# Scores and bias of a unit's first head group issued one slot earlier, and an output projection that waits half by half

## The chip, the cores and the metric

The kernel runs on one core of a Trainium2 chip. The metric is the device time of one execution in microseconds (us). Five engines run streams of their own and meet at semaphores: TensorE (PE, its weight loads are shown as PEld), VectorE (DVE), ScalarE (ACT), GpSimd (POOL) and SyncE (SP, which issues the transfers here).

## The reference, cut to what matters

Two attention layers stand one after the other, over 64 batch elements of 128 rows and 512 columns, with 16 heads of 64, one shared key and value head, a null key and value, a causal mask, and a layer norm before the projections and behind the output projection:

```
xn = layernorm(x) * g_in                       # 128 x 512
q = xn @ Wq ; k, v = xn @ Wkv                  # layer 1: q and k brought to unit length and scaled
sim = q @ concat(null_k, k).T + bias           # bias: a given tensor (layer 0), a small network (layer 1)
attn = softmax(where(causal and mask, sim, -big))
x = x + layernorm((attn @ concat(null_v, v)) @ Wo) * g_out
```

Layer 1 takes the x that layer 0 leaves.

## The kernel before, in words

A *unit* is one batch element in one layer; there are 128. The order of the work is written out by hand, for each engine apart, as a row of *slots*, one unit `u` each. In the slot of `u` the engines do: scores, softmax and values of `u`; the output projection and output norm of the unit before, `v`; the input projections of a later unit or pair of units, `w`; the input statistics of a still later one, `n`. `then` is the unit whose slot comes next. Layer 0's units are projected in pairs, layer 1's one by one. The steady state is a loop of 29 rounds with four slots in each (one more round of the same four stands behind it, then six slots of layer 1's kind):

- `first`: u of layer 1, project the first half of the heads of a layer-0 pair w (`project_pair(w, 0, ...)`);
- `late`: u of layer 0, project one layer-1 unit w (`project`, then `transpose_k`, `transpose_q`);
- `second`: u of layer 1, project the keys and the second half of the heads of the pair;
- `late` again.

The names that the steps below need:

- `scores(u, c)` (L643 on, matmul L673): the scores of head group c (0 or 1) into the PSUM banks `SB[c]`. `SB[0]` is the two banks `Y` and `XT`, which also take the output projection and the transposed input; so the transposes (L543) and `project_out(v, 0, u)` (L708) that come behind wait for `biased[0]`.
- `add_bias(u, c)` (DVE, L1128): adds the masked bias to the scores of group c, from PSUM into `probs`, and raises `biased[c]`. Only then is the bank free.
- `row_max` (DVE, L1134), `exponential` (ACT, L896), `inverse_sum` (DVE, L1139), `divide` (POOL, L1466), `turn` (DVE, L1144): the softmax, in two groups of row blocks; `turned[1]` is its end.
- `values(u)` (matmul L690): 64 small matmuls (32-row tiles) in four steps k, behind `turned`.
- `split_o` on ACT (L902, two halves `o_hi`) and on DVE (L1151, two halves `o_lo`): values out of PSUM. `project_out(v, p)` has three passes of eight matmuls: p = 0 and 1 read `o_hi`, p = 2 reads `o_lo`.
- `take_half` (ACT, L866): copies half of a pair's projected queries from PSUM into `qp` and raises `half_copied`. A layer-0 unit's scores read `qp`.
- `rstd_of_input` (ACT, L835 and L837), `input_statistics` (DVE, L1068, L1070), `normalise` (DVE, L1075), `split_x` (ACT L848 or L850, DVE L1081 or L1083: high and low parts of the transposed input), `centre_output` (DVE, L1156 to L1160), `mask_bias` (POOL, L1456).

Before the change each slot begins on PE with `scores(u, 0)`, `scores(u, 1)`, and on DVE with `add_bias(u, 0)`, `add_bias(u, 1)`.

Of the kernel before, what the change touches and what calls it, by code (L numbers as in the profile page):

```python
# [139 lines left out]
BLOCKS = 4  # L140
# [20 lines left out]
def build(nc, x, bias0, null_kv, keep0, keep1, L0, L1, out):  # L161
# [18 lines left out]
    with ctx:  # L180
# [358 lines left out]
        def _(pe):  # L539
# [137 lines left out]
            def values(u):  # L677
                n, filled = side(u)
                wait(pe, v_rep_loaded[n], filled * 16 * 4)
                wait(pe, o_lo_done[1], u.prev)  # L680
                for g in range(len(GROUPS)):
                    wait(pe, turned[g], u.done)
                if not isinstance(u.done, int):
                    pe.sem_inc(pe_passed, 1)
                p_t = probs_t[:, :, :, :, :].rearrange("p (c e) k b i -> p c e k b i", e=2)
                for k in range(BLOCKS):
# [6 lines left out]
                m.then_inc(values_done, 1)  # L693
# [46 lines left out]
            def begin(w, n, n2, then):  # L740
# [8 lines left out]
                transpose_v(w)  # L749

            def first0(u, v, w, n, then):
                scores(u, 0)
# [9 lines left out]
                values(u)  # L762

            def second0(u, v, w, n, then):
                pe.wait_ge(diag_computed, 1)
                scores(u, 0)
# [10 lines left out]
                values(u)  # L777

            def late0(u, v, w, n, loads, then, pairs_done):
                pe.wait_ge(lo_done, 3 * KC)  # L780
                pe.wait_ge(bias1_copied, BLOCKS)
# [3 lines left out]
            def first(u, v, w, n, then):  # L785
                scores(u, 0)
# [7 lines left out]
                values(u)  # L794

            def second(u, v, w, n, then):
                scores(u, 0)
# [7 lines left out]
                project_pair(w, 1, (3,), u)  # L805
                wait(pe, pair_v_ready, w.pdone * 2)
                values(u)

            def late(u, v, w, n, loads, then, pairs_done):
                if u:  # L810
                    scores(u, 0)
                    scores(u, 1)
# [11 lines left out]
                if u:  # L824
                    if not w:
                        wait(pe, o_lo_done[0], u.prev)
                    values(u)
# [4 lines left out]
        def _(act):  # L832
# [220 lines left out]
        def _(dve):  # L1053
# [70 lines left out]
            def add_bias(u, c):  # L1124
                if c == 0:
                    wait(dve, masked_bias_done, u.done)
# [125 lines left out]
            def begin(w, n, n2, then):  # L1252
# [312 lines left out]
```

## Time and profile before

| | |
|---|---|
| median of 3 runs | 2237.0 us (2236.79 to 2238.55) |
| the profiled execution's own time | 2237.55 us, its span 2235.8 us |
| busy in the span | PE 93%, PEld 83%, DVE 73%, ACT 70%, POOL 46% |
| granted TensorE clock | 0.989 of full speed |
| a round of four slots, from the transposes of one `first` to those of the next | 67.51 us (1064.08 to 1131.59) |

Busy time is summed over the execution, so a share says how much of the span an engine worked, not whether it was waited for. PE's records overlap by their pipelined ends; the idle times that the views put beside an instruction are counted from the end of the one before.

### The profile page before, as it was taken

Reading aid. Unit: us, or ns where it says so; the run is one execution under the profiler, and the core shown is the slowest. Engines: PE = TensorE matmul, PEld = TensorE weight load, DVE = VectorE, ACT = ScalarE, POOL = GpSimd, SP = SyncE. Lnnn points to the kernel's source line nnn. Section 1 sums busy time; section 2 is a strip of 40 time slices with the busy share of each in tenths; the row PEclk is TensorE's granted clock in tenths of the full one; section 3 lists DMA queues with packets and bytes.
Section 4 is the critical chain, followed back from the end, with each engine's and each line's share of the span. In section 5 each row is a group of like instructions: output and inputs, shape, how many; then the busy total and the mean of one; then the engine's idle time right before and its main releaser. Section 6 shows DMA issues by size and latency. Waiting matters only on the chain.

```text
span 2235.8 us, 72261 instructions
## 1 busy us (share of the span) xinstructions
PE 2077.9 (93%) x26395; PEld 1859.0 (83%) x26395; DVE 1625.1 (73%) x3422; ACT 1562.1 (70%) x6241; POOL 1028.6 (46%) x1510
## 2 busy tenths in 40 slices
PE   4799999999999999999999999999999999999987
PEld 4788888888888888888888888888888888888876
DVE  5677777777777777777777777777777777777775
ACT  4567777777777677776777776676677677677775
POOL 3444444444544544544444444444444444444453
PEclk8899999999999999999999999999999999999998
DMA  8112222212222212222222221122221122221111
GB/s 257 41 55 61 70 61 61 67 55 60 72 61 61 67 55 60 72 61 61 62 59 61 72 61 56 58 68 59 69 64 55 57 68 61 63 68 58 59 59 45
DMA packets 183034, 147.47 MB, mean 66 GB/s; under 512 B 121440, under 2 KB 125616, under 8 KB 182992
## 3 DMA queue, kind: packets, MB, share of 16 engines
q1 hardware_dynamic: 181248, 145.77, 21.8%
q0 software_dynamic: 688, 1.14, 0.3%
q8 instruction: 26, 0.43, 0.1%
q10 hardware_dynamic: 1056, 0.00, 0.0%
q14 instruction: 16, 0.13, 0.0%
HBM read 98.56 MB, written 37.77 MB: 61 GB/s over the span
## 4 chain that ended last, share of the span: by engine, by line
PE 62%; DVE 16%; DMA 6%; issue 5%; ACT 4%; SPq 3%; POOL 2%; DVEq 0%; POOLq 0%; ACTq 0%
PE psum L708 21%; PE psum L581 15%; PE psum L615 11%; DVE probs L1128 6%; PE psum L690 6%; PE psum L673 4%; DMA xa<-in_x_dram 4%; ACT probs L896 4%; DVE neg_max L1134 2%; POOL probs L1466 2%; SPq L443 2%; PE psum L592 2%; DVE o_lo L1151 2%; DMA v_kept<-v_diff 2%; DVE bn_in L1068 2%
## 5 line engine op out<-in xcount | busy, mean ns | idle before, releaser
L896 ACT ACTIVATE probs<-probs,neg_max 128x129 f32<-128x129 f32 (+3 forms) x2048 | 712.7, 352 | 66.7 <-DVE neg_max L1134 66.7
L1456 POOL TENSOR_TENSOR masked_bias<-bias,pad_neg 128x516 f32<-128x516 f32 (+3 forms) x512 | 403.9, 821 | 220.1 <-DVE probs L1128 214.1
L1466 POOL TENSOR_TENSOR probs<-probs,den_inv 128x512 f32<-128x512 f32 (+3 forms) x512 | 368.0, 740 | 214.2 <-DVE den_inv L1139 214.1
L1478 POOL TENSOR_TENSOR y_out<-y_out,res 128x512 f32<-128x512 f32 x128 | 164.7, 1287 | 538.0 <-ACT y_out L860 538.0
L896 ACT ACTIVATION_READ_ACCUMULATOR probs<-probs,neg_max 128x1 f32 x2048 | 386.7, 189 | 0.0
L1144 DVE STREAM_TRANSPOSE probs_t<-probs 128x512 f32<-128x512 f32 (+3 forms) x512 | 230.0, 487 | 138.3 <-POOL probs L1466 137.2
L708 PE MATMUL psum<-wo_hi,o_hi 128*128 128x512 f32 x1024 | 275.3, 411 | 19.9 <-DVE probs L1128 18.5
L1128 DVE TENSOR_TENSOR probs<-psum,masked_bias 128x648 f32<-128x648 f32 x256 | 201.5, 828 | 118.3 <-PE psum L673 118.0
L708 PE MATMUL psum<-wo_hi,o_lo 128*128 128x512 f32 x1024 | 264.9, 400 | 21.0 <-DVE o_lo L1151 21.0
L708 PE MATMUL psum<-wo_lo,o_hi 128*128 128x512 f32 x1024 | 260.6, 396 | 0.0
L708 PEld LDWEIGHTS psum<-wo_hi,o_lo 128*128 128x128 f32 x1024 | 187.5, 188 | 77.1 <-DVE o_lo L1151 25.9
L1134 DVE TENSOR_REDUCE neg_max<-probs 128x4 f32<-128x516 f32 (+3 forms) x512 | 233.8, 483 | 13.4
L708 PEld LDWEIGHTS psum<-wo_hi,o_hi 128*128 128x128 f32 x1024 | 186.5, 192 | 58.8 <-issue 17.4
L708 PEld LDWEIGHTS psum<-wo_lo,o_hi 128*128 128x128 f32 x1024 | 192.0, 188 | 41.4
L902 ACT ACTIVATE o_hi<-psum,null_v_col 128x512 fp32r<-128x512 f32 x256 | 162.1, 684 | 45.8 <-PE psum L690 40.7
L690 PE MATMUL psum<-probs_t,v_rep 32*64 32x256 f32 (+3 forms) x8192 | 183.9, 308 | 8.8 <-DVE probs_t L1144 8.7
L866 ACT COPY qp<-psum 128x512 f32<-128x512 f32 x128 | 74.3, 582 | 164.6 <-PE psum L581 164.6
L1151 DVE SCALAR_TENSOR_TENSOR o_lo<-psum,null_v_col,o_hi 128x512 fp32r<-128x512 f32 x256 | 187.3, 741 | 1.8 <-ACT o_hi L902 1.8
L690 PEld LDWEIGHTS psum<-probs_t,v_rep 32*64 32x64 f32 x8192 | 156.5, 132 | 38.3 <-issue 20.3
L581 PE MATMUL psum<-xp_hi,w_hi 128*128 128x256 f32 x1024 | 168.6, 286 | 5.6 <-ACT w_hi L934 4.3
L615 PE MATMUL psum<-w_hi,x_hi 128*128 128x384 f32 x768 | 167.0, 339 | 0.0
L615 PE MATMUL psum<-w_lo,x_hi 128*128 128x384 f32 x768 | 166.8, 339 | 0.0
(133 smaller groups left out, 3986.8 us busy)
## 6 DMA issues: line engine op xcount, KB each, us to landing
res<-in_x_dram SPq DMA_DIRECT2D x64, 256.0 KB, 2.7
v_rep<-v_kept SPq DMA_DIRECT2D x512, 32.0 KB, 1.8
x_of<-y_out SPq DMA_DIRECT2D x64, 256.0 KB, 2.1
res<-x_of SPq DMA_DIRECT2D x64, 256.0 KB, 2.7
out_dram<-y_out SPq DMA_DIRECT2D x64, 256.0 KB, 2.1
xa<-in_x_dram SPq DMA_DIRECT2D x63, 256.0 KB, 2.7
xa<-x_of SPq DMA_DIRECT2D x63, 256.0 KB, 2.9
q_aside<-qp SPq DMA_DIRECT2D x32, 256.0 KB, 3.1
```

The costliest lines, as they stand in the source:

```text
L581: m = nc.tensor.matmul(o, ws[0][:, c, q:q + P], xs[:, c, :, :].rearrange("p b i -> p (b i)"), start=(n == 0), stop=(n == 3 * KC - 1))
L615: m = nc.tensor.matmul(Q[b][:, 0:hi - lo], xs[:, c * P:(c + 1) * P], ws[1][:, c, lo:hi], start=(n == 0), stop=(n == 3 * KC - 1))
L690: m = nc.tensor.matmul(o, v_rep[n][strip, k, :], p_t[strip, :, e, k, k:, :].rearrange("p c b i -> p c (b i)"), start=(k == 0), stop=(k == ...
L708: m = nc.tensor.matmul(Y[:, 0:D], os[:, k * P:(k + 1) * P], ws[u.layer][:, j, :], start=(p == 0 and k == 0), stop=(p == 2 and k == PAIRS - 1))
L896: x_ = nc.scalar.activation(s, s, ACT.Exp, bias=neg_max[:, b, n:n + 1], accum_out=den[:, b, n:n + 1])
L1128: nc.vector.tensor_tensor(pairs(probs, c), SB[c][:, :, 0:ROW], pairs(masked_bias, c), ALU.add).then_inc(biased[c], 1)
L1134: nc.vector.tensor_reduce(neg_max[:, b, :], block(probs, b), AX.X, ALU.max, negate=True).then_inc(max_done[b], 1)
L1144: m = nc.vector.transpose(probs_t[:, :, 0:b + 1, b, :], block(probs, b)[:, :, 1:].rearrange("p n (k r) -> p n k r", r=R))
L1151: nc.vector.scalar_tensor_tensor(part_of(o_lo), psum[:, 4 + 2 * f:6 + 2 * f, 0:2 * P], null_v_col[:, 0:1], part_of(o_hi).bitcast(F32), ALU ...
L1456: m = nc.gpsimd.tensor_tensor(block(masked_bias, b), block(bias[u.layer], b), pad_neg[u.layer][:, 0:WIDTH[b]].unsqueeze(1).to_broadcast([P ...
L1466: m = nc.gpsimd.tensor_tensor(some, some, den_inv[:, b, :].unsqueeze(2).to_broadcast([P, 4, n]), ALU.mult)
L1478: nc.gpsimd.tensor_tensor(y_out[:, :], y_out[:, :], res[:, :], ALU.add).then_inc(out_done, 1)
```

## The change

PE: `scores(then, 0)` is issued in the slot before that of its unit: in `first` and `second` ahead of `values(u)`, in `late` between the second and the third of the four steps of `values(u)`. A slot then begins with `scores(u, 1)`. `project_out` waits for the first half of `o_hi` or `o_lo` ahead of its first matmul and for the second half ahead of its fifth.

DVE: `add_bias(then, 0)` is the last instruction of the slot before (with waits for `turned`, since it overwrites `probs`). In `first` the two `split_o` come ahead of the last two `row_max`; in `second` the second `split_o` comes ahead of the last `row_max`.

ACT: in `first`, `split_x(w.even)` comes ahead of `rstd_of_input(w.odd)`.

```diff
             def project_out(u, p, now=None):
+                arrived = {0: o_hi_done, 2: o_lo_done}
                 if p == 0:
-                    for b in range(2):
-                        wait(pe, o_hi_done[b], u.done)
                     wait(pe, y_taken, u.prev)
                     if now:
                         wait(pe, biased[0], now.done)
-                if p == 2:
-                    for b in range(2):
-                        wait(pe, o_lo_done[b], u.done)
                 for k in range(PAIRS):
                     j = k // 2 + 4 * (k % 2)
+                    if p in arrived and k % 4 == 0:
+                        wait(pe, arrived[p][k // 4], u.done)
...
             def first(u, v, w, n, then):          # PE
-                scores(u, 0)
                 scores(u, 1)
...
                 project_pair(w, 0, (0, 1, 2, 3), u)
-                values(u)
+                scores(then, 0)
+                values(u, range(BLOCKS))
...
             def second(u, v, w, n, then):         # PE
-                scores(u, 0)
                 scores(u, 1)
...
                 project_pair(w, 1, (3,), u)
+                scores(then, 0)
                 wait(pe, pair_v_ready, w.pdone * 2)
-                values(u)
+                values(u, range(BLOCKS))
...
             def late(u, v, w, n, loads, then, pairs_done):   # PE
-                    scores(u, 0)
                     scores(u, 1)
...
-                    values(u)
+                    values(u, range(2))
+                if then:
+                    scores(then, 0)
+                if u:
+                    values(u, range(2, BLOCKS))
...
             def first(u, v, w, n, then):          # ACT
+                split_x(w.even)
                 rstd_of_input(w.odd)
-                split_x(w.even)
...
             def add_bias(u, c):                   # DVE
                 if c == 0:
+                    for g in range(len(GROUPS)):
+                        wait(dve, turned[g], u.prev)
                     wait(dve, masked_bias_done, u.done)
...
             def first(u, v, w, n, then):          # DVE; second and late lose and gain the same add_bias
                 input_statistics(w.odd)
-                add_bias(u, 0)
                 add_bias(u, 1)
...
                 split_x(w.even)
+                split_o(v, 0)
+                split_o(v, 1)
                 row_max(u, 2)
                 row_max(u, 0)
-                split_o(v, 0)
-                split_o(v, 1)
...
                 normalise(n)
+                add_bias(then, 0)
```

The start-up slots (`begin`, `first0`, `second0`, `late0`) are changed in the same way.

PE where a `late` slot ends and the next begins, before: four steps of values (L690), then both groups of scores (L673).

```order
L690 MATMUL psum<-probs_t,v_rep 64x256 x8
L690 MATMUL psum<-probs_t,v_rep 64x2x96 x8
L690 MATMUL psum<-probs_t,v_rep 64x2x64 x8
L690 MATMUL psum<-probs_t,v_rep 64x2x32 x8
L673 MATMUL psum<-keys,q_t 64x129 x4
L673 MATMUL psum<-keys,q_t 64x97 x4
L673 MATMUL psum<-keys,q_t 64x65 x4
L673 MATMUL psum<-keys,q_t 64x33 x4
L673 MATMUL psum<-keys,q_t 64x129 x4
L673 MATMUL psum<-keys,q_t 64x97 x4
L673 MATMUL psum<-keys,q_t 64x65 x4
L673 MATMUL psum<-keys,q_t 64x33 x4
```

The same place after the change (values are L691 there).

```order
L691 MATMUL psum<-probs_t,v_rep 64x256 x8
L691 MATMUL psum<-probs_t,v_rep 64x2x96 x8
L673 MATMUL psum<-keys,q_t 64x129 x4
L673 MATMUL psum<-keys,q_t 64x97 x4
L673 MATMUL psum<-keys,q_t 64x65 x4
L673 MATMUL psum<-keys,q_t 64x33 x4
L691 MATMUL psum<-probs_t,v_rep 64x2x64 x8
L691 MATMUL psum<-probs_t,v_rep 64x2x32 x8
L673 MATMUL psum<-keys,q_t 64x129 x4
L673 MATMUL psum<-keys,q_t 64x97 x4
L673 MATMUL psum<-keys,q_t 64x65 x4
L673 MATMUL psum<-keys,q_t 64x33 x4
```

The first group of the next unit's scores now stands in the middle of the values.

PE at the end of `second`, before, with the semaphores waited for: the last tile of the pair's projection (L581), the values, then the scores of the next unit, of layer 0, which wait for the copied queries.

```order
L581 MATMUL psum<-xp_lo,w_hi 128x8x32 x4
L64 REGISTER_ALU
L64 ISA [waits pair_v_ready]
L690 MATMUL psum<-probs_t,v_rep 64x256 [waits turned1,turned0,v_rep_loaded2,o_lo_done1]
L690 MATMUL psum<-probs_t,v_rep 64x256 x7
L690 MATMUL psum<-probs_t,v_rep 64x2x96 x8
L690 MATMUL psum<-probs_t,v_rep 64x2x64 x8
L690 MATMUL psum<-probs_t,v_rep 64x2x32 x8
L64 REGISTER_ALU [waits half_copied1,half_copied0]
L673 MATMUL psum<-kv_t,qp 64x129 [waits k_high_loaded,y_taken]
```

After the change (the scores go on for 13 more matmuls, and the values stand behind them).

```order
L581 MATMUL psum<-xp_lo,w_hi 128x8x32 x4
L64 REGISTER_ALU
L64 REGISTER_ALU [waits half_copied1,half_copied0]
L673 MATMUL psum<-kv_t,qp 64x129 [waits k_high_loaded,y_taken]
L673 MATMUL psum<-k_high,qp 64x129
L673 MATMUL psum<-kv_t,qp 64x129
```

The wait for `half_copied` now comes directly behind the projection whose result is copied, and no longer behind the values.

DVE at the beginning of `first`, before.

```order
L1128 TENSOR_TENSOR probs<-psum,masked_bias 128x648 [waits scores_done0,masked_bias_done]
L1128 TENSOR_TENSOR probs<-psum,masked_bias 128x648 [waits scores_done1]
L1134 TENSOR_REDUCE neg_max<-probs 128x4 [waits biased1,biased0]
L1075 TENSOR_SCALAR xn<-xa,mv_in,rstd_in 128x512 [waits xt_done,rstd_in_done]
L1134 TENSOR_REDUCE neg_max<-probs 128x4
L1083 TENSOR_TENSOR xp_lo<-psum,xp_hi 128x4x128 [waits x_hi_done]
L1134 TENSOR_REDUCE neg_max<-probs 128x4 x2
L64 REGISTER_ALU
L1151 SCALAR_TENSOR_TENSOR o_lo<-psum,null_v_col,o_hi 128x512 [waits o_hi_done0]
L1151 SCALAR_TENSOR_TENSOR o_lo<-psum,null_v_col,o_hi 128x512 [waits o_hi_done1]
```

After the change (add_bias is L1134, row_max L1140, normalise L1079, split_x L1087, split_o L1157).

```order
L1134 TENSOR_TENSOR probs<-psum,masked_bias 128x648 [waits scores_done1]
L1140 TENSOR_REDUCE neg_max<-probs 128x4 [waits biased1,biased0]
L1079 TENSOR_SCALAR xn<-xa,mv_in,rstd_in 128x512 [waits xt_done,rstd_in_done]
L1140 TENSOR_REDUCE neg_max<-probs 128x4
L1087 TENSOR_TENSOR xp_lo<-psum,xp_hi 128x4x128 [waits x_hi_done]
L64 REGISTER_ALU
L1157 SCALAR_TENSOR_TENSOR o_lo<-psum,null_v_col,o_hi 128x512 [waits o_hi_done0]
L1157 SCALAR_TENSOR_TENSOR o_lo<-psum,null_v_col,o_hi 128x512 [waits o_hi_done1]
L1140 TENSOR_REDUCE neg_max<-probs 128x4 x2
```

One addition has left the beginning of the slot, and the two `o_lo` stand ahead of the last two maxima.

## Rows read from the trace of the kernel before

**Rows 1.** Page: the span, then busy time, share and instructions of each engine.

```profile
span 2235.8 us, 72261 instructions
PE 2077.9 (93%) x26395; PEld 1859.0 (83%) x26395; DVE 1625.1 (73%) x3422; ACT 1562.1 (70%) x6241; POOL 1028.6 (46%) x1510
```

**Rows 2.** Page: the chain of work that ended last, shares by engine.

```profile
PE 62%; DVE 16%; DMA 6%; issue 5%; ACT 4%; SPq 3%; POOL 2%; DVEq 0%; POOLq 0%; ACTq 0%
```

**Rows 3.** Waits, PE: us in total, times, longest.

```profile
PE psum L543 <- DVE probs L1128: 53.3, 94, 7.2
...
PE psum L708 <- DVE o_lo L1151: 21.0, 30, 0.9
...
PE psum L708 <- DVE probs L1128: 18.5, 32, 3.6
```

**Rows 4.** Timeline, PE, slot `first`: start, us, instruction, count, [idle before, releaser].

```profile
1062.11 1.44 PE L673 MATMUL psum<-keys,q_t 64*64 64x129 f32 x64 [0.50 <-issue]
1064.08 0.65 PE L543 MATMUL psum<-ident,xn 128*128 128x128 f32 x4 [0.53 <-DVE probs L1128]
...
1068.31 0.60 PE L543 MATMUL psum<-ident,xn 128*128 128x128 f32 x4
1069.69 2.11 PE L708 MATMUL psum<-wo_hi,o_lo 128*128 128x512 f32 x8 [0.79 <-DVE o_lo L1151]
...
1077.41 1.42 PE L690 MATMUL psum<-probs_t,v_rep 32*64 32x256 f32 x64
```

**Rows 5.** Timeline, PE, end of `second` and beginning of `late`.

```profile
1109.74 0.64 PE L581 MATMUL psum<-xp_hi,w_lo 128*128 128x256 f32 x4
1110.21 0.63 PE L581 MATMUL psum<-xp_lo,w_hi 128*128 128x256 f32 x4
1110.77 1.42 PE L690 MATMUL psum<-probs_t,v_rep 32*64 32x256 f32 x64
1112.17 0.29 PE L673 MATMUL psum<-kv_t,qp 64*64 64x129 f32 x1
...
1112.78 0.30 PE L673 MATMUL psum<-kv_t,qp 64*64 64x129 f32 x1
...
1114.08 0.65 PE L543 MATMUL psum<-ident,xn 128*128 128x128 f32 x4 [0.47 <-DVE probs L1128]
```

**Rows 6.** Timeline, ACT, end of the same `second`.

```profile
1110.79 0.29 ACT L835 ACTIVATE ln_in<-mv_in,eps_col 128x1 f32<-128x1 f32 x1 [1.20 <-DVE mv_in L1070]
...
1111.22 0.57 ACT L866 COPY qp<-psum 128x512 f32<-128x512 f32 x1
```

**Rows 7.** Timeline, PE, window of 0.06 us around the last matmuls of those values.

```profile
1111.87 0.32 PE L690 MATMUL psum<-probs_t,v_rep 32*64 32x64 f32 x6
```

**Rows 8.** Timeline, DVE, slot `first`.

```profile
1062.10 0.70 DVE L1068 BATCH_NORM_STATS2 bn_in<-xa 128x6 f32<-128x512 f32 x1 [0.25 <-DMA xa<-in_x_dram]
...
1063.12 1.57 DVE L1128 TENSOR_TENSOR probs<-psum,masked_bias 128x648 f32<-128x648 f32 x2
...
1065.41 1.24 DVE L1075 TENSOR_SCALAR xn<-xa,mv_in,rstd_in 128x512 f32<-128x512 f32 x1
...
1067.49 0.74 DVE L1134 TENSOR_REDUCE neg_max<-probs 128x4 f32<-128x388 f32 x2
1068.15 1.39 DVE L1151 SCALAR_TENSOR_TENSOR o_lo<-psum,null_v_col,o_hi 128x512 fp32r<-128x512 f32 x2
...
1075.38 0.74 DVE L1144 STREAM_TRANSPOSE probs_t<-probs 128x384 f32<-128x384 f32 x2
```

**Rows 9.** Timeline, DVE, ACT and PE, end of a `late` slot and beginning of `second`.

```profile
1095.09 0.75 DVE L1160 SCALAR_TENSOR_TENSOR y_out<-y_out,mv_out,g_out 128x512 f32<-128x512 f32 x1
...
1095.76 1.27 ACT L902 ACTIVATE o_hi<-psum,null_v_col 128x512 fp32r<-128x512 f32 x2
...
1095.64 1.44 PE L673 MATMUL psum<-keys,q_t 64*64 64x129 f32 x64
1097.58 2.12 PE L708 MATMUL psum<-wo_hi,o_hi 128*128 128x512 f32 x8 [0.50 <-DVE probs L1128]
```

More of the change, by code:

```diff
@@ L675, in scores, with values @@
                 m.then_inc(scores_done[c], 1)
-            def values(u):
+            def values(u, blocks):
                 n, filled = side(u)
[L679 to L684, printed above, removed]
+                if 0 in blocks:
+                    wait(pe, v_rep_loaded[n], filled * 16 * 4)
+                    wait(pe, o_lo_done[1], u.prev)
+                    for g in range(len(GROUPS)):
+                        wait(pe, turned[g], u.done)
+                    if not isinstance(u.done, int):
+                        pe.sem_inc(pe_passed, 1)
                 p_t = probs_t[:, :, :, :, :].rearrange("p (c e) k b i -> p c e k b i", e=2)
-                for k in range(BLOCKS):
+                for k in blocks:
                     for e in range(2):
@@ L692, in values @@
                                                  start=(k == 0), stop=(k == BLOCKS - 1))
-                m.then_inc(values_done, 1)
+                if BLOCKS - 1 in blocks:
+                    m.then_inc(values_done, 1)
             def project_out(u, p, now=None):
+                arrived = {0: o_hi_done, 2: o_lo_done}
                 if p == 0:
-                    for b in range(2):
-                        wait(pe, o_hi_done[b], u.done)
                     wait(pe, y_taken, u.prev)
@@ L793, in first @@
                 project_pair(w, 0, (0, 1, 2, 3), u)
-                values(u)
+                scores(then, 0)
+                values(u, range(BLOCKS))
             def second(u, v, w, n, then):
-                scores(u, 0)
                 scores(u, 1)
@@ L805, in second @@
                 project_pair(w, 1, (3,), u)
+                scores(then, 0)
                 wait(pe, pair_v_ready, w.pdone * 2)
-                values(u)
+                values(u, range(BLOCKS))
             def late(u, v, w, n, loads, then, pairs_done):
                 if u:
-                    scores(u, 0)
                     scores(u, 1)
@@ L826, in late @@
                         wait(pe, o_lo_done[0], u.prev)
-                    values(u)
+                    values(u, range(2))
+                if then:
+                    scores(then, 0)
+                if u:
+                    values(u, range(2, BLOCKS))
             run_units(pe, begin, first0, second0, late0, first, second, late, NB)
@@ L1125, in add_bias @@
                 if c == 0:
+                    for g in range(len(GROUPS)):
+                        wait(dve, turned[g], u.prev)
                     wait(dve, masked_bias_done, u.done)
@@ L1304, in first0 @@
                 low_parts((2 * KC + 1,))
+                add_bias(then, 0)
             def second0(u, v, w, n, then):
                 low_parts((2 * KC + 2,))
-                add_bias(u, 0)
                 add_bias(u, 1)
@@ L1326, in second0 @@
                 low_parts((2 * KC + 3, 3 * KC))
+                add_bias(then, 0)
             def late0(u, v, w, n, loads, then, pairs_done):
@@ L1334, in first @@
                 input_statistics(w.odd)
-                add_bias(u, 0)
                 add_bias(u, 1)
@@ L1352, in first @@
                 normalise(n)
+                add_bias(then, 0)
             def second(u, v, w, n, then):
-                add_bias(u, 0)
                 add_bias(u, 1)
@@ L1360, in second @@
                 row_max(u, 2)
+                split_o(v, 1)
                 row_max(u, 0)
-                split_o(v, 1)
                 inverse_sum(u, 0)
@@ L1371, in second @@
                 normalise(n)
+                add_bias(then, 0)
             def late(u, v, w, n, loads, then, pairs_done):
                 if u:
-                    add_bias(u, 0)
                     add_bias(u, 1)
@@ L1412, in late @@
                 centre_output(v)
+                if then:
+                    add_bias(then, 0)
             run_units(dve, begin, first0, second0, late0, first, second, late, NB)
```

4 lines of the change are left out of this document (2 added, 2 removed).

## The prediction

> **What bounds the kernel now.** I read the page first: PE is busy for 2077.9 of 2235.8 us [rows 1], and the chain that ended last runs 62% over PE and 16% over DVE [rows 2]. So PE sets the time, and 158 us of its idle time are all that a change of order can win. The list of waits says who causes the part that this change touches: 53.3 us of transposes waiting for the bias addition in 94 waits, 18.5 us of output projections waiting for it in 32, and 21.0 us of output projections waiting for `o_lo` in 30 [rows 3]. The longest of the first two lists, 7.2 and 3.6 us, lie in the start-up slots. Without them 46.1 us in 93 and 14.9 us in 31 are left, 0.49 us at each slot's beginning, four times a round; the `o_lo` wait comes once a round, in `first`.
>
> The timeline shows how it arises. In `first`, the scores begin at 1062.11 and are all issued and finished by 1063.55, but the transposes behind them start at 1064.08, 0.53 us later, because the addition for group 0 must first clear the banks [rows 4]. Later in that slot the third output pass starts 0.79 us late [rows 4], since DVE ran the two `o_lo` only from 1068.15 to 1069.54 [rows 8].
>
> **Removed.** With `add_bias(then, 0)` done before the slot begins, the waits at slot beginnings go: 46.1 + 14.9 = 61.0 us. That needs DVE to be in time. At a `late` slot's end the last instruction of the output norm ends at 1095.84 [rows 9]; an addition behind it takes about 0.8 (1.57 for two [rows 8]), so `biased[0]` comes at about 1096.7, while the output pass started at 1097.58 before [rows 9] and is wanted at about 1097.4 after. The cover is some 0.5 us.
>
> A stall costs a little more than its idle row, since a stream of matmuls overlaps: between groups of one kind the next starts before the recorded end of the last (1109.74 + 0.64 = 1110.38, next at 1110.21, so 0.17), and where the tile shape changes by 0.07 (1110.21 + 0.63 = 1110.84, values at 1110.77) [rows 5]. So 124 beginnings give 124 x 0.07 = 8.7 us more, and 30 `o_lo` waits 30 x 0.17 = 5.1.
>
> For the `o_lo` wait I lay out the slot after, with T the start of its transposes. DVE first ends the moved addition, then needs 1.02 us for the input statistics (1062.10 to 1063.12, [rows 8]). PE meanwhile issues the last two steps of the values, crosses the loop's branch (0.50 [rows 4]) and issues the second group of scores (0.61, from 1112.17 to 1112.78, [rows 5]), so DVE starts `add_bias(u, 1)` at about T + 0.25 and ends it at T + 1.05. From there row_max takes 0.72 (1064.69 to 1065.41), then normalise, one row_max and split_x 2.08 (1065.41 to 1067.49) and the two `o_lo` 1.39 [rows 8]. The first `o_lo` is ready at T + 4.55, the second at T + 5.25. PE wants the first at T + 4.66 (the odd transposes at T + 4.23, as from 1064.08 to 1068.31, and 0.60 less the overlap of 0.17 for them [rows 4]) and the second four matmuls later, half of a pass of 2.11 - 0.17 [rows 4], at T + 5.6. Both are just in time, the first by 0.1 us. I take the whole 21.0 us; the other bound is nothing.
>
> Sum removed: 61.0 + 21.0 + 8.7 + 5.1 = 95.8 us.
>
> **Added.** *Changes of tile shape.* Scores use 64-row tiles, values 32-row, the rest 128. `first` and `second` gain one change each (scores alone ahead of the values), a `late` slot two (scores amid the values): six a round, 180 in 30 rounds, some 12 more in the single `late` slots, 192. The projection's groups start 0.47 us apart, the values start 0.56 behind the last of them [rows 5]: a change costs 0.09. From values to scores: six matmuls are in flight from 1111.87 [rows 7]; 64 in 1.40 us is 0.02 each, so the last is issued near 1111.97, and the scores start at 1112.17 [rows 5]: 0.20, less 0.02, is 0.18, with the scores' own waits in it. From scores to values no row stands; I take 0.13 for all, midway, with ends of 0.09 and 0.20. 192 x 0.13 = 25 us.
>
> The Trainium skill (TensorEngine Tiling (Array Packing), Key Properties) speaks against the change here: it says that a change of tiling mode drains TensorE. The trace agrees that a change costs something but shows the next matmul 0.07 us ahead of the last one's recorded end [rows 5]. A full drain at each change is among the rivals.
>
> *A new wait in `second`.* This is the part that the change does to itself. `scores(then, 0)` for a layer-0 unit needs the second `take_half`, which ACT can only begin when PE has finished the last projected tile. Before, the values hid it: they were issued at 1110.77, and ACT ended the copy at 1111.22 + 0.57 = 1111.79 [rows 5, 6]. ACT is also held until 1110.79 by the statistics of another unit, which it takes first [rows 6]. Now PE stands until about 1111.85 (0.06 for the signal, as the statistics' release to ACT): 1.08 us, with the values, `split_o` and the next slot queued behind. Nothing else of PE can slip in. 31 x 1.08 = 33.5 us.
>
> *The half-wise wait.* It matters where no transposes stand between: `late` to `second`. ACT began `o_hi` 0.12 us behind the first score (1095.64, 1095.76) and takes about 0.68 for a half of its 1.27 [rows 9]; with 0.06 the half is ready 0.86 behind the values, and the second group of scores covers 0.61 + 0.15. 0.10 x 30 = 3 us. A wait for both halves would have cost 0.6 more each; so the split of the waits is needed, and that of `o_lo` likewise.
>
> DVE, ACT and POOL get no new work. The start-up waits should shrink by two additions, about 2 us (bounds nothing and 10.8).
>
> **Sum.** 95.8 - 25 - 33.5 - 3 + 2 = 36 us, 1.2 us of a round of 67.5. The profiled execution took 2237.55, 0.55 above the median of the runs; against the median of 2237.0 that gives **2201 us**.
>
> **Rivals.**
> *The new wait stays away* (ACT copies earlier because its statistics come earlier): + 33.5, 2168. For it: ACT waits 1.20 us for DVE's statistics there [rows 6]. Against: those wait for the transposed v of the same projection, and no line of `second` on ACT moves.
> *DVE is late in `first`*: the margin of 0.1 us is less than what one stretched instruction costs (normalise took 1.24 us here beside POOL's bias [rows 8]). If the wait for `o_lo` or for `split_x` stays as long as it was, 26 us are not won: 2227; half of it gives 2214.
> *A full drain at each change of shape*: the last small matmul of the values takes 0.22 (six in 0.32, 0.02 apart [rows 7]); 192 x (0.22 - 0.02) is 38 us in place of 25: 2214. That is what the Trainium skill's sentence on mode switching (TensorEngine Tiling (Array Packing), Key Properties), taken strictly, would come to.
> *Slower: the softmax of `first` ends too late.* `turn` ended at 1075.38 + 0.74 = 1076.12 [rows 8], and the values came at 1077.41 [rows 4], 1.29 us of cover. After the change exponentials start 0.4 us later behind T (the addition's end at T + 1.05 against 1064.69 - 1064.08 = 0.61), PE comes 0.96 earlier and 0.74 later by the scores ahead of the values: 0.7 us of cover. From 0.7 us of delay PE waits for `turned`; from 1.85 the gain is gone; 2.5 would give 30 x 0.65 = 20 us more than before, 2257. For it: two maxima now stand behind `o_lo`. Against: ACT reaches them only after eight exponentials of group 0.
> *No effect*: gains and new waits cancel (every small bound at its bad end): 2233 to 2241.
>
> **How the numbers follow.** My forecast has a chance of 0.52; new wait absent 0.08; DVE late 0.14; full drain 0.14; cancelled 0.05; slower 0.07. Within 0.2% of the median, about what a measurement of this kernel can tell, is 2232.5 to 2241.5: faster 0.88, same 0.05, slower 0.07. The range leaves out the slower case, the cancelled one and the far end of the absent wait: 2170 to 2226.
>
> **What would show it.** Right: the idle times for the bias addition at slot beginnings are gone or below 0.1 us, so is the one for `o_lo`; in `second` one new wait of PE's scores on ACT's copy (L866 of before), about 1.1 us, 30 times; a round of about 66.3 us. The values' group in `late` is longer by its two changes, 0.2 to 0.4. Wrong: a wait of the values on `turn`, of the odd transposes on `split_x`, or of slot beginnings on the bias addition as before; or no wait on the copy.

## The result, and the profile after

The changed kernel takes 2399.4 us (median of 4, 2398.89 to 2401.68) against 2237.6: a ratio of 1.0725, interval 1.0706 to 1.0744. That is 162 us more, where the forecast had been 36 us less (2201). The profiled execution has a span of 2397.1 us.

The page after: span, busy time of the engines, and the queue that carries instructions (packets, MB, share of the 16 DMA engines). Before, that queue had 26 packets and 0.43 MB.

```profile
span 2397.1 us, 72132 instructions
...
PE 2148.4 (90%) x26395; PEld 1914.7 (80%) x26395; DVE 1624.3 (68%) x3422; ACT 1557.8 (65%) x6241; POOL 1030.0 (43%) x1510
...
q8 instruction: 278, 4.55, 0.9%
```

The list of PE's waits after (us in total, times, longest), beside [rows 3]:

```profile
PE psum L673 <- issue: 153.8, 58, 5.0
PE psum L673 <- ACT qp L870: 42.0, 30, 4.4
...
PE psum L708 <- ACT o_hi L906: 1.5, 4, 0.9
...
PE psum L543 <- DVE probs L1134: 1.1, 2, 0.7
```

The three waits of [rows 3] are gone, as meant: 53.3 us in 94 is 1.1 in 2, and the two rows of L708 on `o_lo` and on the bias addition stand no more. The predicted new wait on ACT's copy is there: less its start-up case, 42.0 - 4.4 = 37.6 us in 29, 1.30 each. But one row that nobody had moved has grown from 14.2 us in 29 to 153.8 in 58: scores that wait for "issue", for nothing that the profile shows. Before, it read

```profile
PE psum L673 <- issue: 14.2, 29, 0.9
```

The timeline of PE after, in the slot `first`, beside [rows 4]:

```profile
1064.84 1.07 PE L673 MATMUL psum<-keys,q_t 64*64 64x129 f32 x32 [4.63 <-issue]
1065.84 1.11 PE L543 MATMUL psum<-ident,xn 128*128 128x128 f32 x4
1066.61 3.05 PE L708 MATMUL psum<-wo_hi,o_hi 128*128 128x512 f32 x8
1069.49 2.02 PE L708 MATMUL psum<-wo_lo,o_hi 128*128 128x512 f32 x8
...
1071.71 2.11 PE L708 MATMUL psum<-wo_hi,o_lo 128*128 128x512 f32 x8
```

This is the loop's restart. It cost 0.50 before [rows 4] and costs 4.63 now. The transposes then take 1.11 us in place of 0.65, the first output pass 3.05 in place of 2.11. The windows of PE (length, busy times with instructions in brackets, granted clock, DMA share, GB/s) say why: of two whole rounds and of two stretches of the second of them,

```profile
985.84:1059.86 74.02, 67.26 (x840) 59.99 (x833) 49.75 (x106) 47.92 (x194) 31.53 (x46) 0.95 0.21 59
1059.86:1132.91 73.05, 66.03 (x840) 59.03 (x832) 49.83 (x105) 47.93 (x194) 31.61 (x46) 0.98 0.21 59
1059.86:1065.00 5.14, 0.51 (x37) 0.40 (x25) 1.61 (x3) 1.87 (x3) 1.53 (x2) 1.00 0.12 36
1065.00:1070.00 5.00, 5.00 (x47) 4.27 (x43) 3.49 (x6) 2.98 (x14) 3.05 (x4) 0.66 0.27 81
```

PE stood nearly idle for 5 us, and the granted clock of the 5 us behind that is 0.66 of full speed, a mean of its two levels: from 1065.25 to 1068.66 the same view gives 0.50, the level of 1.2 GHz. A round is 73 to 74 us long, and 67.5 before. In the second of these rounds the transfers are (queue, packets, MB, share):

```profile
q1 hardware_dynamic: 5408, 4.20, 19.6%
q8 instruction: 9, 0.15, 0.9%
```

Nine instruction packets of 16 KB (4.55 MB / 278) move in a round; before, the same view of a round lists no such queue. The records of the loop's own line say whose program it is (count, then shortest, median and longest duration in ns; PEldq is PE's sequencer), after and then before:

```profile
L91 PEldq COMPARE_BRANCH  x29: 83/4820/5112, 180.5 to 2234.4; - x29
```

```profile
L91 PEldq COMPARE_BRANCH  x29: 76/208/239, 184.5 to 2073.2; - x29
```

The branch that sends PE back to its loop's beginning takes 4.82 us in place of 0.21; the branches of the other engines take 0.04 to 0.07 in both. So the first theory after the result was that PE reads its loop's program again in every round.

### The profile page after: what moved, and what is told of

Read it like the earlier page. It is cut to its first block, busy times and chain, and to the rows that moved or that the text cites. A ratio compares the mean times of both kernels' runs of the same rounds, so it can differ in the third digit from the quotient of the medians.

```text
span 2397.1 us, 72132 instructions
## 1 busy us (share of the span) xinstructions
PE 2148.4 (90%) x26395; PEld 1914.7 (80%) x26395; DVE 1624.3 (68%) x3422; ACT 1557.8 (65%) x6241; POOL 1030.0 (43%) x1510
## 3 DMA queue, kind: packets, MB, share of 16 engines
q8 instruction: 278, 4.55, 0.9%
## 4 chain that ended last, share of the span: by engine, by line
PE 84%; issue 8%; DVE 2%; ACT 2%; SPq 1%; POOL 1%; DMA 1%; DVEq 0%; POOLq 0%; ACTq 0%
PE psum L708 31%; PE psum L615 17%; PE psum L581 12%; PE psum L673 9%; PE psum L691 7%; PE psum L543 3%; PE psum L632 2%; PE psum L592 2%; DVE bn_in L1072 1%; SPq L386 1%; ACT qp L870 1%; POOL probs L1474 1%; POOL masked_bias L1464 0%; ACT ln_in L839 0%; ACT probs L900 0%
## 5 line engine op out<-in xcount | busy, mean ns | idle before, releaser
L1134 DVE TENSOR_TENSOR probs<-psum,masked_bias 128x648 f32<-128x648 f32 x256 | 213.0, 832 | 313.3 <-PE psum L673 312.8
L708 PE MATMUL psum<-wo_hi,o_hi 128*128 128x512 f32 x1024 | 307.0, 447 | 3.6 <-issue 2.1
L673 PE MATMUL psum<-keys,q_t 64*64 64x129 f32 (+3 forms) x4096 | 129.6, 265 | 156.0 <-issue 152.9
L708 PE MATMUL psum<-wo_hi,o_lo 128*128 128x512 f32 x1024 | 262.5, 398 | 0.0
L708 PE MATMUL psum<-wo_lo,o_hi 128*128 128x512 f32 x1024 | 262.4, 398 | 0.0
L673 PEld LDWEIGHTS psum<-keys,q_t 64*64 64x64 f32 x4096 | 112.1, 153 | 182.9 <-issue 180.5
L708 PEld LDWEIGHTS psum<-wo_hi,o_hi 128*128 128x128 f32 x1024 | 209.0, 215 | 47.6 <-issue 4.1
L1140 DVE TENSOR_REDUCE neg_max<-probs 128x4 f32<-128x516 f32 (+3 forms) x512 | 236.1, 482 | 13.7
L708 PEld LDWEIGHTS psum<-wo_lo,o_hi 128*128 128x128 f32 x1024 | 195.4, 192 | 43.1
L708 PEld LDWEIGHTS psum<-wo_hi,o_lo 128*128 128x128 f32 x1024 | 190.0, 188 | 44.0
L691 PE MATMUL psum<-probs_t,v_rep 32*64 32x256 f32 (+3 forms) x8192 | 195.8, 309 | 10.1 <-DVE probs_t L1150 10.0
L1157 DVE SCALAR_TENSOR_TENSOR o_lo<-psum,null_v_col,o_hi 128x512 fp32r<-128x512 f32 x256 | 187.2, 740 | 1.7 <-ACT o_hi L906 1.7
L691 PEld LDWEIGHTS psum<-probs_t,v_rep 32*64 32x64 f32 x8192 | 145.5, 132 | 37.2 <-issue 21.5
L581 PE MATMUL psum<-xp_hi,w_hi 128*128 128x256 f32 x1024 | 169.1, 287 | 5.3 <-ACT w_hi L938 4.0
```

The source lines that it names most:

```text
L581: m = nc.tensor.matmul(o, ws[0][:, c, q:q + P], xs[:, c, :, :].rearrange("p b i -> p (b i)"), start=(n == 0), stop=(n == 3 * KC - 1))
L673: m = nc.tensor.matmul(block(SB[c][:, e, :], b)[r:r + TR, :], queries(u, c, half, b)[:, r:r + TR], k, start=True, stop=True)
L691: m = nc.tensor.matmul(o, v_rep[n][strip, k, :], p_t[strip, :, e, k, k:, :].rearrange("p c b i -> p c (b i)"), start=(k == 0), stop=(k == ...
L1134: nc.vector.tensor_tensor(pairs(probs, c), SB[c][:, :, 0:ROW], pairs(masked_bias, c), ALU.add).then_inc(biased[c], 1)
L1140: nc.vector.tensor_reduce(neg_max[:, b, :], block(probs, b), AX.X, ALU.max, negate=True).then_inc(max_done[b], 1)
L1157: nc.vector.scalar_tensor_tensor(part_of(o_lo), psum[:, 4 + 2 * f:6 + 2 * f, 0:2 * P], null_v_col[:, 0:1], part_of(o_hi).bitcast(F32), ALU ...
```

## The experiments

**Theory A**: PE's loop no longer stays in its instruction memory, because of where it stands in PE's program; the moved work has nothing to do with it. **Rival B**: the moved scores stall PE. **Rival C**: clock or start-up. The loop has 1713 PE instructions before and 1705 after, so it did not grow; but it begins 60 instructions later (1593 in place of 1533, counted in the compiled program), since the start-up slots now hold one more group of scores ahead of it.

### Padding: the same loops at other places

Waits on a semaphore that is long raised were put on PE at the start of the program; two of them make one instruction. The first three kernels differ by their number alone.

```diff
             def begin(w, n, n2, then):            # PE
-                pe.wait_ge(ident_done, 1)
+                for _ in range(374):              # 186 instructions more; 122: 60 more; 514: 256 more
+                    pe.wait_ge(ident_done, 1)
```

The changed kernel, 186 later. 

> The changed kernel with 186 more PE instructions (waits on a semaphore that is long raised) at the start of the program, where PE waits for the first input anyway; nothing in the loop differs. Theory A (position): the trace after shows nine transfers of the instruction queue of 16 KB each in every round of the loop and a stall of 4.63 us at each restart, before it shows none, so the time is lost to fetching PE's loop again, and this depends on where the loop stands in PE's program. Then a shift by 186 instructions, which gives the loop's beginning about the remainder that lies in the middle of the good range if the loop must lie within seven blocks of 256 instructions, ends the fetches: about 2200 us, 26 to 30 instruction packets. Rival B (the moved work itself, or its order, stalls PE): 2399 us as after. Rival C (the padding disturbs only the start): 2399 plus up to 10.

The kernel before, 60 later. 

> The kernel before with 60 more PE instructions at the start, so that its loop begins at exactly the position of the changed kernel's loop (1593 instructions behind the program's first). Nothing of the change is in it. Theory A: it fetches its loop again in each round as the changed kernel does, with a stall of 4 to 5 us at each restart: 29 rounds of 5.5 to 7 us more, 2395 to 2440 us, some 260 to 280 instruction packets. Rival B (the moved work stalls PE): 2237 us and 26 packets.

The changed kernel, 256 later. 

> The changed kernel with 256 more PE instructions at the start, a whole 16 KB block, so that the loop keeps its place within the blocks. Theory A in the form that the place within a block decides: 2399 us and some 280 packets, as after. A in the form that padding of any size (or a later start) helps, or that the loop's absolute place decides: 2200. Rival B: 2399.

Measured: 2204.4 us (ratio to before 0.9852, 0.9835 to 0.9868), 2394.2 (1.0693, 1.0675 to 1.0711) and 2415.3 (1.0789, 1.0771 to 1.0807). The pages' queue rows, of the first and the second (the third's reads like the second's):

```profile
q8 instruction: 27, 0.44, 0.1%
```

```profile
q8 instruction: 279, 4.57, 0.9%
```

This decides for A, and against B and C. The kernel before, with nothing of the change in it, becomes as slow as the changed one when its loop begins at the same place, and stalls in the same way:

```profile
995.28 2.60 PE L673 MATMUL psum<-keys,q_t 64*64 64x129 f32 x64 [5.13 <-issue]
```

The changed kernel becomes faster than before when its loop is moved off that place; a move by 256 leaves the packets as they are. So the place modulo 256 instructions decides. The 16 us that the third kernel lies above 2399 are within what its padding delays: PE's first matmul came at 6.32 us after the change, at 21.68 with 186 padding instructions and at 29.5 with 256.

In the first padded kernel, the timeline at the restart and at the next end of a `late` slot, and the window of a whole round:

```profile
1049.34 0.59 PE L691 MATMUL psum<-probs_t,v_rep 32*64 32x128 f32 x32
1050.02 0.82 PE L673 MATMUL psum<-keys,q_t 64*64 64x129 f32 x32
1050.78 0.66 PE L543 MATMUL psum<-ident,xn 128*128 128x128 f32 x4
1051.19 2.11 PE L708 MATMUL psum<-wo_hi,o_hi 128*128 128x512 f32 x8
1053.14 2.02 PE L708 MATMUL psum<-wo_lo,o_hi 128*128 128x512 f32 x8
...
1079.47 1.01 PE L691 MATMUL psum<-probs_t,v_rep 32*64 32x256 f32 x32
1080.41 0.82 PE L673 MATMUL psum<-keys,q_t 64*64 64x129 f32 x32
1081.17 0.59 PE L691 MATMUL psum<-probs_t,v_rep 32*64 32x128 f32 x32
1081.68 0.82 PE L673 MATMUL psum<-keys,q_t 64*64 64x129 f32 x32
```

```profile
1049.54:1115.46 65.92, 64.31 (x840) 57.61 (x837) 49.07 (x105) 47.82 (x194) 31.52 (x46) 1.00 0.22 64
```

The restart leaves 0.09 us (1049.34 + 0.59 to 1050.02). Against this round the one of 73.05 above is 7.13 us longer, and three rows of the trace after make that up: the stall, 4.63 - 0.09 = 4.54; the stretch from the first scores to the second output pass, at the lower clock, 4.65 (1064.84 to 1069.49) in place of 3.12 (1050.02 to 1053.14), 1.53; and a second gap in the scores amid the values:

```profile
1099.94 0.24 PE L673 MATMUL psum<-keys,q_t 64*64 64x33 f32 x2 [1.09 <-issue]
```

Together 7.16.

### Where the border lies

Two more places of the kernel before (62 waits in place of one for 30 instructions, 342 for 170), and the changed kernel at its own place with a shorter loop; one execution each.

> The kernel before shifted by 30 PE instructions: its loop begins 27 behind a multiple of 256 (counted in the compiled program; the multiple is that of the count, and what the chip places ahead of the program is not known). Loops at remainders 253 and 243 stayed without fetches, at 57 they were fetched each round. If the loop must lie within seven blocks of 256, as 1713 instructions can in 80 of 256 places, and the unknown lead is 31 to 82 instructions, either answer is possible and halves the open range: 2237 and 27 packets if the lead is below 53, 2395 and 279 if above.

> The kernel before shifted by 170: remainder 167. If a loop of 1713 instructions must lie within seven blocks of 256, this place needs eight for any lead of 31 to 82: fetched in each round, about 279 packets, 2395 to 2415 us. If not the number of blocks but something else about the place decides (say a beginning in the first quarter of a block is bad, any other good), no fetches: 2237 to 2255.

```diff
             def project_out(u, p, now=None):
+                if p == 1 and not isinstance(u.done, int):
+                    return
```

> The changed kernel, unshifted, with the second pass of the output projection left out inside the loop alone (that part of the result is then missing), so that the loop begins at the same place and is 64 instructions shorter (1642 in place of 1706). If the loop must lie within seven blocks, 1642 instructions can do so from 151 places of 256, and the place that was bad for 1706 is good for a lead up to 94: no fetches, 27 packets; time: 2194 less 29 x 4 passes x 1.94 us (2.11 less the overlap of 0.17) = 225 us: 1965 to 1975. If the place alone decides, whatever the length: some 280 packets and 2399 less 225 = 2174.

Measured: 2257.2, 2449.5 and 2159.4 us; 54, 279 and 26 packets. The short loop is not fetched, at a place where the long one is: length counts together with place. Its time missed my number by 190 us and lies near the rival's 2174, but the 26 packets rule that rival out. I had only taken PE's work off: with less of it PE waits for others, in the list of waits (first two lines) as in the chain that ended last

```profile
PE psum L543 <- DVE xp_lo L1089: 51.0, 30, 11.2
PE psum L632 <- DVE q_sb L1121: 47.2, 59, 1.0
...
PE 41%; DVE 19%; issue 17%; POOL 12%; ACT 7%; SPq 2%; DMA 1%; DVEq 1%; POOLq 0%; ACTq 0%
```

The shift by 30 gave what neither theory had: a mixture within one execution. Three of its 28 full rounds fetch, the others don't. Windows of four neighbouring rounds:

```profile
931.90:999.52 67.62, 64.31 (x846) 57.67 (x832) 49.96 (x106) 48.14 (x196) 31.55 (x46) 1.00 0.21 62
999.52:1073.47 73.95, 66.45 (x833) 59.66 (x824) 49.81 (x106) 48.03 (x195) 31.55 (x46) 0.95 0.21 59
1073.47:1147.00 73.53, 66.96 (x833) 60.12 (x824) 49.49 (x106) 48.04 (x194) 31.57 (x46) 0.95 0.20 59
1147.00:1214.46 67.46, 64.18 (x844) 57.56 (x832) 49.81 (x106) 48.02 (x195) 31.54 (x46) 1.00 0.21 62
```

The middle two have nine instruction packets each, the outer two none. The same program pays about 6.2 us for a round that is fetched (73.74 on average against 67.54).

The shift by 170 is fetched as expected, but took 2449.5 us where I had put at most 2415. Its loop stalls twice where it begins, and its granted clock is 0.937 where the shift by 60 has 0.951:

```profile
1018.14 1.02 PE L673 MATMUL psum<-keys,q_t 64*64 64x129 f32 x14 [4.04 <-issue]
1021.45 2.04 PE L673 MATMUL psum<-keys,q_t 64*64 64x97 f32 x50 [2.29 <-issue]
```

All places together, with the loop's beginning modulo 256, its length in PE instructions, and its end in blocks of 256 when 52 instructions are taken to stand ahead of the program:

| kernel | begins at | length | end in blocks | packets in the execution |
|---|---|---|---|---|
| before | 253 | 1713 | 6.88 | 26 |
| after | 57 | 1705 | 7.09 | 278 |
| after, +186 | 243 | 1705 | 6.81 | 27 |
| before, +60 | 57 | 1713 | 7.12 | 279 |
| after, +256 | 57 | 1705 | 7.09 | 279 |
| before, +30 | 27 | 1713 | 7.00 | 54 |
| before, +170 | 167 | 1713 | 7.55 | 279 |
| after, short loop | 57 | 1641 | 6.84 | 26 |

The end in blocks counts from the start of the block in which the loop begins, so 7.09 means that the loop touches eight blocks. Loops that touch seven stay; those that touch eight are fetched again, with nine packets a round; the one that ends on the border goes both ways. The 52 is fitted to the row of 54 packets; the seven is what the rows bear out, since a loop of 1641 to 1713 instructions touches seven or eight blocks wherever it begins. The gaps behind the restart support the fit. Counted in the records of the trace, the second stall of the shift by 170 stands ahead of the loop's 35th instruction; with the 52 that is place 253 in its block (167 + 52 + 34). In the five kernels that fetch (after, after +256, before +30, +60 and +170), all 75 later gaps of over 0.6 us in which PE waits for no semaphore stand at place 252 or 253, at loop instructions as far apart as 34, 143, 912, 942 and 1423: three or four ahead of a border.

The Trainium skill (Runtime: NRT & Kernel Launch, Instruction fetch mechanics) says that the instruction memory is refilled in blocks of 16 KiB, 256 instructions, and that a taken branch whose target lies outside of the current window of two such pages stalls for a fetch. The trace agrees with the blocks and with the stall: packets of 16 KB, and 4.63 us at the restart. It does not agree with a window of two: loops that touch seven blocks restart without a packet. The page gives TensorE 2048 instructions, eight blocks; by that a loop of eight blocks could have stayed, and by the runs it did not.

### The parts of the change

In the second padded version of the change, the scores of the next unit stand behind the values in `second`.

```diff
             def second(u, v, w, n, then):         # PE
-                scores(then, 0)
                 wait(pe, pair_v_ready, w.pdone * 2)
                 values(u, range(BLOCKS))
+                scores(then, 0)
```

> The changed kernel shifted by 186 instructions, and in slot second the scores of the next unit's first group stand behind the values again instead of ahead of them (the addition stays at the slot's end). Against the shifted kernel: if the wait of those scores for ACT's copy (1.3 us a round in the trace after) is a real cost there, it goes and 30 x (1.3 less a late addition of up to 0.5) = 24 to 39 us are won: 2161 to 2176 if the shifted kernel takes 2200. If the addition then comes too late for the transposes of the slot behind, or the wait is only passed on: within 5 us of the shifted kernel. Rival B for both: about 2399.

Measured: 2175.4 us (0.9721, 0.9704 to 0.9737), 29 us less than with the scores ahead of the values. The row on ACT's copy shrinks to its start-up case; of the 1.30 us a round, 0.5 come back as a wait of the next slot's transposes for the addition. The two rows in this kernel:

```profile
PE psum L543 <- DVE probs L1135: 17.4, 32, 2.1
...
PE psum L673 <- ACT qp L871: 4.4, 1, 4.4
```

The same with the padding spread over the start-up, at five places where PE waits anyway; one of them:

```diff
             def first0(u, v, w, n, then):         # PE
                 scores(u, 1)
                 transpose_even(w, u)
+                for _ in range(180):              # 90 instructions
+                    pe.wait_ge(ident_done, 1)
                 transpose_odd(w)
```

> The fourth kernel (shift by 186, in second the scores behind the values), with the same 186 padding instructions spread over five places of the start-up at which PE waits anyway: 48 at the beginning, 12 and 6 around the second transposes, 90 ahead of the odd transposes of first0 (idle 11.9 us there in the trace after), 30 ahead of the last scores of second0 (idle 4.4 us). In the first padded kernel the loop's first branch came 10.3 us later than in the kernel after (190.8 against 180.5), since 186 waits at the very beginning take 21.7 us and hide only 6. If the padding is what costs that, about 10 us go: 2163 to 2168; if those 10 us come from elsewhere: 2175 as the fourth kernel.

Measured: 2163.3 us (0.9669, 0.9656 to 0.9682), 12 less. The padding did cost those 10 us, so the first padded kernel would have taken about 2194 without it.

The two halves of the diff, each alone: first the small parts without any moved scores (half-wise waits, order on DVE and ACT), then the move without the small parts (with the padding spread as above; its loop begins 190 later).

```diff
             def first(u, v, w, n, then):          # DVE, as in the change; second and ACT likewise
-                row_max(u, 2)
-                row_max(u, 0)
                 split_o(v, 0)
                 split_o(v, 1)
+                row_max(u, 2)
+                row_max(u, 0)
```

> The kernel before with the small parts of the change alone: the half-wise waits of the output projection, o_lo ahead of the last maxima on DVE, split_x first on ACT; no scores and no addition moved. Its loop starts at instruction 1529, four ahead of the kernel before, so that I expect no fetching. If the o_lo wait (21.0 us in 30) goes and with it the overlap at 30 resumptions (5 us): 2212. If it is hidden by the bias wait at the slot's beginning, or the maxima's lateness costs as much: 2233 to 2240.

```diff
             def project_out(u, p, now=None):      # the changed kernel, with the waits of before
+                if p == 0:
+                    for b in range(2):
+                        wait(pe, o_hi_done[b], u.done)
+                if p == 2:
+                    for b in range(2):
+                        wait(pe, o_lo_done[b], u.done)
-                    if p in arrived and k % 4 == 0:
-                        wait(pe, arrived[p][k // 4], u.done)
```

> The changed kernel with the scores and the addition moved, but without the small parts (output projection waits for both halves, the old order of o_lo and maxima, the old order on ACT); shifted by 190 with the padding spread. The full change without its padding stands near 2194. If the parts simply add, the 26 us of the o_lo wait come back: 2216 to 2222. If the earlier start of the slot makes DVE later against PE (PE wants o_lo earlier while DVE still has the maxima ahead), the o_lo wait grows from 0.70 to 1.2 us or more: 2232 to 2245, no gain at all over before. If the order no longer matters: 2195.

Measured: 2206.0 us (0.9865, 0.985 to 0.988) and 2262.4 (1.011, 1.0094 to 1.0125). Neither fetches (26 and 27 packets). The second lies outside of all three outcomes that I had put. The parts do not add: the small ones alone win 31 us, the move alone loses 26, both together win some 43 (2194). With the move alone, these waits stand in the list:

```profile
PE psum L673 <- ACT qp L882: 42.1, 30, 4.6
PE psum L710 <- ACT o_hi L918: 25.1, 33, 1.5
PE psum L710 <- DVE o_lo L1169: 17.6, 30, 1.2
```

The `o_lo` wait did not grow, though I had put growth for a time with no gain (0.56 a round, before 0.70). What grew is the wait for both halves of `o_hi`, in all four slots. Without the addition's wait at the slot's beginning, the first output pass comes so early that ACT is not done. In `first` of this kernel the pass starts 0.22 us behind the recorded end of the transposes:

```profile
1072.05 0.66 PE L543 MATMUL psum<-ident,xn 128*128 128x128 f32 x4
1072.93 2.10 PE L710 MATMUL psum<-wo_hi,o_hi 128*128 128x512 f32 x8 [0.23 <-issue]
...
1106.10 2.11 PE L710 MATMUL psum<-wo_hi,o_hi 128*128 128x512 f32 x8 [0.74 <-ACT o_hi L918]
```

In the first padded kernel it starts 0.25 ahead of that end (1050.78 + 0.66 against 1051.19); that is 0.47 in `first`. There ACT ended the second half of `o_hi` 0.34 ahead of the pass (1071.32 + 1.27 in its own timeline), and two more instructions of PE's sequencer stand in between, so only a part of the 0.47 is ACT's. In `second` the wait is 0.74 in place of 0.20. The two `late` slots lose 0.32 and 0.33 in the same way, and `o_lo` 0.56 with its lost overlap of 0.17. Sum 2.39 us a round; the rounds are 68.34 and 65.92 long, 2.42 apart.

Last, two edits on the way to a better kernel, both on the version with spread padding: the scores of `second` amid the values; and beside that, ACT's second copy ahead of the other unit's statistics. First both, then the place of the scores alone.

```diff
             def second(u, v, w, n, then):         # PE
-                values(u, range(BLOCKS))
-                scores(then, 0)
+                values(u, range(2))
+                scores(then, 0)
+                values(u, range(2, BLOCKS))
...
             def second(u, v, w, n, then):         # ACT, only in the first of the two
-                rstd_of_input(n)
                 take_half(w, 1, 1)
+                rstd_of_input(n)
```

> As the kernel beside it, but in second the scores of the next unit stand amid the values (behind the second of four steps, as in late), and ACT takes the second take_half ahead of the other unit's input statistics. The theory that ACT's copy is held until 1110.79 by those statistics, and that the addition's lateness at the next slot's beginning (17.4 us in 32 waits in the fourth kernel) is what is left to win: 0.5 us a round less two changes of tile shape at about 0.1, 8 to 12 us below the kernel beside it. Rival: the statistics, now later, make normalise and with it the addition on DVE late by the same 0.5: no gain or a loss of up to 10.

> As the kernel with the scores of second amid the values, but with ACT's order of the change (the other unit's statistics ahead of the second take_half). The kernel with both edits took 2156.8, the one with the scores behind the values 2163.3. If the copy is held by the statistics, PE waits for it amid the values: the copy ended about 1.05 us behind the projection's last group in the trace before, the values' first two steps cover 0.95, so 0.1 to 0.3 us a round, 3 to 9 us: 2160 to 2166, and the order on ACT is what makes the edit pay. If the values' first half covers the copy in either order: 2157, and the place of the scores alone is the gain.

Measured: 2156.8 us (0.9639, 0.9626 to 0.9652) and 2166.0 (0.9679, 0.9666 to 0.9692). With both, the addition's wait falls from 17.3 us in 32 to 1.5 in 2 and no wait on the copy comes in its place beyond the start-up case. With the old order on ACT, PE waits amid the values, 10.3 us in 29:

```profile
PE psum L673 <- ACT qp L881: 14.8, 30, 4.5
```

So the place of the scores pays only with the copy taken first. 2156.8 is the best of all, 3.6% below the kernel before, though 6.5 us under the version with the scores behind the values, not the 8 to 12 that I had put.

## Why the prediction was wrong

**The step that failed** is "crosses the loop's branch (0.50 [rows 4])". I took the cost of the loop's restart from the row of before as fixed, and had no term and no rival for PE's supply with instructions. The change put 60 PE instructions more ahead of the loop; that alone moved the loop's end past seven blocks, and each round then paid 7.4 us: 28 rounds x 7.4 (73.35 against 65.92 on average) = 208 us. The kernel before with 60 idle instructions shows it without the change. The order of instructions, which the prediction used, would have shown the 60; no row of the trace of before shows that a restart can cost more.

**What stood up, once the loop stays.** The first padded kernel took 2204.4, about 2194 without its padding, against the 2201 of the forecast; a round won 1.53 us (67.45 to 65.92) where I had 1.2. That the two times lie so close is in part luck: the terms below miss by 2 to 12 us each, in both directions.

- *Waits removed.* The 61.0 us at slot beginnings and the 21.0 of `o_lo` are gone in full. DVE was in time in `first`; so the rival of a late DVE fell.
- *Changes of tile shape.* 0.13 each was right. From the start of a `late` slot's values to the recorded end of the next slot's second group of scores it was 2.79 us (1094.29 to 1095.64 + 1.44 [rows 9]); in the first padded kernel 3.03 (1079.47 to 1081.68 + 0.82), with two changes more: 0.12 each. The rival of a full drain fell. The values of before:

```profile
1094.29 1.42 PE L690 MATMUL psum<-probs_t,v_rep 32*64 32x256 f32 x64
```

- *The new wait in `second`* was there, 1.30 a round against 1.08, some 4 us more than the sum had. The signal to ACT that I took as 0.06 reads 0.04 in the trace of before (`mv_in` ends at 1110.57 + 0.18, ACT begins at 1110.79), which changes the sum by 0.6 us. Scores behind the values would have saved 29 us.
- *The half-wise wait.* 3 us predicted for the residue; measured 6.0 (0.20 in each of 30 `second` slots), the row below less 1.5 of the start-up. I had said that a wait for both halves would cost 0.6 more in one slot of four. With the move alone the first pass came 1.66 later over all four slots, 48 us in 29 rounds: mis-sized by much, though it did not enter the sum. The order on ACT and DVE was set back in the same run, so the price of the wait alone is not shown.

```profile
PE psum L708 <- ACT o_hi L907: 7.5, 33, 0.9
```

- *The restart* itself got cheaper where nothing is fetched: 0.09 in place of 0.50, some 12 us in all, for which the sum had no term. It outweighs the 0.3 a round by which the new wait and the half-wise wait came out larger; about 0.2 of what the round won beyond my 1.2 stays unaccounted for. Why the restart is cheaper is open; in the program after, the loop's second block of register instructions stands behind the first scores and no longer ahead.
- *Softmax of `first` too late*: the values wait on `turn` only twice in the whole execution, so not in the rounds. Start-up: the loop's first branch came 4.0 us earlier (180.5 for 184.5); I had 2.

So the forecast of the schedule was good to 7 us, and the forecast of the kernel was wrong by 198.

## What to carry to other kernels

When an edit moves instructions into or out of the code ahead of a hot loop, look at the instruction queue's packets, before and after: a loop that is nearly as long as what the engine keeps can fall out of it by its place alone, and the loss hides under waits for "issue" at the loop's first instruction. Shift the loop by padding in an idle place and time again before you judge the edit. And test the parts of a change apart: here a move that loses alone gains with a finer wait behind it.

## What the runs showed of the hardware

- PE's loop of 1705 to 1713 instructions stays without fetches over 29 rounds where it touches seven blocks of 256, and is fetched whole, nine packets of 16 KB a round, where it touches eight; at the border both happen within one execution (54 packets). The blocks are counted with 52 instructions ahead of the program, a fit to the row of 54 packets that the places of the later gaps support to within four.
- A restart that must fetch left PE idle for 4.0 to 5.1 us in the rounds shown (4.63 after the change, 5.13 with 60 and 4.04 with 170 more), and after the change the granted clock of the next 5 us was 0.66: another 1.5 us. Where the loop begins just ahead of a border (the shift by 170), a second stall of 2.29 us followed at once.
- 186 instructions of satisfied waits at the very beginning held PE's first matmul from 6.32 to 21.68 us, so they cost about 0.1 us an instruction.
